# Norm stages of a four-layer kernel: the copies of the turned features shared by VectorE and ScalarE, and one dummy product behind the turns instead of four

## Chip, cores and metric

One Trainium2 chip, one of its cores. The metric is the device time of one execution in microseconds. A time without anything said is counted from the start of the profiled execution's span.

## What is computed

The input is 4 sequences of 256 tokens with 256 features in float32. Four layers follow each other, and each one has the same frame:

```python
xn = _layernorm(x, axis=-1)
s = _Lk_attn_ref(xn, ...)
g = _silu(_Lk_ffn_ref(xn, ...))
x = x + s * g
```

The mixers are, in order, a gated linear recurrence, a selective scan, a 16-head attention and a latent attention; the feed-forward parts are a mixture with 8 experts, a squared-relu network with a layer norm, a mixture with 16 experts and capacity 128, and a network with 4-bit weights. Only the layer norm ahead of layer 0 and of layer 2 is touched here. It takes each token's mean and variance over its 256 features, `(x - m) / sqrt(v + 1e-5)`.

## The kernel before, in words

The 1024 tokens lie as 8 tiles (`NT`) of 128 tokens, one token on a partition (`x_tok`, `xn_tok`). The products need the features on the partitions, so each norm also makes `xnT`, two tiles (`KD`) of 128 features by 1024 tokens, worked on in two halves of 512 tokens.

`norm_stage` (line 78) is called four times: by layer 0 (first norm), layer 1 (second, with `rms_to`, which makes a second scaled and turned copy), layer 2 (third) and layer 3 (fourth, with `beside`, a function that adds work on weights). The first and the third have neither. They are one block each, in which every engine has its own written-out program, and a block ends when all engines have reached its end (line 106 is where that shows up as a releaser in the trace).

- **SyncE** issues the layer's weight loads (lines 110 to 115) and waits for the first part of them (line 117). In the third norm these are four small loads it waits for and four later ones (`Wq`, `Wq_swap`, `cos`, `sin`), for which GpSimd waits in the stage behind.
- **VectorE** makes mean and variance from the statistics taken earlier (line 127), the reciprocal root with ScalarE's help (lines 129, 176, 131), and then the 8 normed token tiles (line 137).
- **TensorE** first runs two dummy products (line 155, `keep_busy` at line 239: a product of the identity with itself, 512 columns wide, whose result nobody reads; in float32 each is two instructions in the trace). Then it turns the 8 token tiles, two turns each, into four PSUM banks (line 160); the semaphore `turned` counts the tiles. Behind them come more dummy products (line 171): one in layer 0, four in layer 2.
- **ScalarE** waits for the first four turned tiles, copies two banks of 512 columns to `xnT`, waits for the other four and copies the other two (lines 182 to 186): four copies in all, in one queue.

`xnT_ready` is counted by these copies, but nobody waits for it: the stage behind reads `xnT` because the block has ended.

Behind the first norm comes `recurrent_layer_stage` (line 275), whose TensorE begins with the input product of `xnT` (line 506) and the router's small products (line 481). Behind the third comes `route_stage`: its TensorE begins with 16 instructions for the logits of 16 experts (line 1717), then the key product (line 1724), logits again, keys again, and then the queries (line 1699), which wait until GpSimd has turned the query weights by the position tables (lines 1658 and 1662). VectorE waits for the logits (line 1821) and then finds each token's experts. Its SyncE issues the next loads at once (line 1638 on).

Of the kernel before, what the change touches and what calls it, by code (L numbers as in the profile page):

```python
# [31 lines left out]
KD = D // P  # L32
HALF = N // 2
# [44 lines left out]
def norm_stage(nc, layer, x_tok, stats, xn_tok, xnT, ident, banks, loads, late=None, parity=False, issued=None, rms_to=None,  # L78
               beside=None):

    with ExitStack() as ctx:
        m = Core(nc, ctx).scope(ctx)
        mean_var = m.sbuf(f"mean_var{layer}", [P, NT, 2])
        var = m.sbuf(f"var{layer}", [P, NT])
        std = m.sbuf(f"std{layer}", [P, NT])  # L90
        rstd = m.sbuf(f"rstd{layer}", [P, NT])
        square = m.sbuf(f"mean_square{layer}", [P, NT])
        rms = m.sbuf(f"rms{layer}", [P, NT])
        norm_steps = nc.alloc_semaphore(f"norm_steps{layer}")
        var_ready = nc.alloc_semaphore(f"norm_var_ready{layer}")
        std_ready = nc.alloc_semaphore(f"norm_std_ready{layer}")
        square_ready = nc.alloc_semaphore(f"mean_square_ready{layer}")
        rms_ready = nc.alloc_semaphore(f"rms_ready{layer}")
        xn_ready = nc.alloc_semaphore(f"xn_ready{layer}")
        turned = nc.alloc_semaphore(f"xn_turned{layer}")  # L100
        xnT_ready = nc.alloc_semaphore(f"xnT_ready{layer}")
        rms_tok_ready = nc.alloc_semaphore(f"rms_tok_ready{layer}")
        rms_turned = nc.alloc_semaphore(f"rms_turned{layer}")
        loaded = nc.alloc_semaphore(f"weights_loaded{layer}")

        with nc.Block(no_gpsimd_drain=True) as block:

            @block.sync
            def _(sp):
                for dst, src in loads:  # L110
                    sp.dma_start(dst, src).then_inc(loaded, DMA)
                if late is not None:
                    for part, sem in zip(late[::2], late[1::2]):
                        for dst, src in part:
                            sp.dma_start(dst, src).then_inc(sem, DMA)
                if loads:
                    sp.wait_ge(loaded, DMA * len(loads))
                if issued is not None:
                    sp.wait_ge(*issued)
                if beside is not None:  # L120
                    beside["sync"](sp)

            @block.vector
            def _(dve):
                steps = Steps(dve, norm_steps)
                for t in range(NT):
                    steps.add(nc.vector.bn_aggr(mean_var[:, t, :], stats[:, t, :]))
                steps.join()
                nc.vector.tensor_scalar(var[:, :], mean_var[:, :, 1], EPS, None, ALU.add).then_inc(var_ready, 1)
                dve.wait_ge(std_ready, 1)  # L130
                steps.do(nc.vector.reciprocal(rstd[:, :], std[:, :]))
                if rms_to is not None:
                    steps.do(nc.vector.tensor_tensor(square[:, :], mean_var[:, :, 1], rstd[:, :], ALU.mult))
                    steps.do(nc.vector.tensor_tensor(square[:, :], square[:, :], rstd[:, :], ALU.mult))
                    nc.vector.tensor_scalar(square[:, :], square[:, :], EPS, None, ALU.add).then_inc(square_ready, 1)
                for t in range(NT):
                    nc.vector.tensor_scalar(
                        xn_tok[:, t, :], x_tok[:, t, :], mean_var[:, t, 0:1], rstd[:, t:t + 1],
                        ALU.subtract, ALU.mult).then_inc(xn_ready, 1)
                if rms_to is not None:  # L140
                    dve.wait_ge(rms_ready, 1)
                    steps.do(nc.vector.reciprocal(square[:, :], rms[:, :]))
                    dve.wait_ge(xn_ready, NT)
                    for t in range(NT):
                        nc.vector.tensor_scalar(rms_to[0][:, t, :], xn_tok[:, t, :], square[:, t:t + 1], None, ALU.mult
                                                ).then_inc(rms_tok_ready, 1)
                if beside is not None:
                    beside["vector"](dve)

            @block.tensor  # L150
            def _(pe):
                if beside is not None:
                    beside["tensor"](pe)
                else:
                    keep_busy(nc, banks[:, 7, :], ident, 2)
                for t in range(NT):
                    pe.wait_ge(xn_ready, t + 1)
                    for k in range(KD):
                        part = xn_tok[:, t, k::2] if parity else xn_tok[:, t, k * P:(k + 1) * P]
                        last = nc.tensor.transpose(  # L160
                            banks[:, KD * (t // 4) + k, (t % 4) * P:(t % 4 + 1) * P], part, ident[:, :])
                    last.then_inc(turned, 1)
                if rms_to is not None:
                    for t in range(NT):
                        pe.wait_ge(rms_tok_ready, t + 1)
                        for k in range(KD):
                            last = nc.tensor.transpose(banks[:, 4 + KD * (t // 4) + k, (t % 4) * P:(t % 4 + 1) * P],
                                                       rms_to[0][:, t, k * P:(k + 1) * P], ident[:, :])
                        last.then_inc(rms_turned, 1)
                elif beside is None:  # L170
                    keep_busy(nc, banks[:, 7, :], ident, 4 if layer else 1)

            @block.scalar
            def _(act):
                act.wait_ge(var_ready, 1)
                nc.scalar.activation(std[:, :], var[:, :], ACT.Sqrt).then_inc(std_ready, 1)
                if rms_to is not None:
                    act.wait_ge(square_ready, 1)
                    nc.scalar.activation(rms[:, :], square[:, :], ACT.Sqrt).then_inc(rms_ready, 1)
                if beside is not None:  # L180
                    beside["scalar"](act)
                for half in range(2):
                    act.wait_ge(turned, 4 * (half + 1))
                    for k in range(KD):
                        nc.scalar.activation(xnT[:, k, half * HALF:(half + 1) * HALF],
                                             banks[:, KD * half + k, :], ACT.Identity).then_inc(xnT_ready, 1)
                if rms_to is not None:
                    act.wait_ge(loaded, DMA * len(loads))
                    for half in range(2):
                        act.wait_ge(rms_turned, 4 * (half + 1))  # L190
                        for k in range(KD):
                            nc.scalar.activation(rms_to[1][:, k, half * HALF:(half + 1) * HALF], banks[:, 4 + KD * half + k, :],
                                                 ACT.Identity, scale=rms_to[2][:, k:k + 1])
# [45 lines left out]
def keep_busy(nc, bank, ident, count):  # L239

    for _ in range(count):
        nc.tensor.matmul(bank.rearrange("p (a b) -> p a b", a=BANK // P), ident[:, :],
                         ident[:, :].unsqueeze(1).broadcast_to([P, BANK // P, P]), start=True, stop=True)
# [2988 lines left out]
```

## Time and profile before

| | |
|---|---|
| median of 3 runs | 985.08 us |
| lowest and highest of them | 983.43 and 988.08 us |
| the profiled execution | 982.9 us |
| its span (first to last instruction) | 981.1 us |
| TensorE busy in the span | 902.4 us, 92% |
| VectorE, ScalarE, GpSimd busy | 666.2, 482.0, 331.2 us |
| mean granted clock of TensorE | 0.985 of full speed |

The profiled execution is a single one and lies 1.8 us outside its span and 2.2 us below the median of the three runs. PE is TensorE's products, PEld its weight loads, DVE is VectorE, ACT ScalarE, POOL GpSimd, SPq the loads and stores that SyncE issues. PEclk is the granted TensorE clock: 1.00 is 2.4 GHz, 0.50 is 1.2 GHz.

### The profile page before, as it was taken

To read this page: it belongs to the slowest core of one execution; us is meant where nothing else is said; L and a number is where in the kernel's file an instruction comes from. 1 tells how busy PE (TensorE), PEld (TensorE's weight loads), DVE (VectorE), ACT (ScalarE), POOL (GpSimd) and SP (SyncE) were. 2 spreads that over 40 slices of the span, in tenths; PEclk is the share of its full clock that TensorE was granted. 3 is DMA by queue.
4 is the path that set the end of the run, shared out by engine and by line. 5 is a ranking of instruction groups with operands and counts; after the bars stand their busy time and mean duration, and the time that the engine had idled before them with its cause. 6 is when DMAs were issued, how large, how long until landed. Compare 5 with 4: busy or idle time off the path is not lost. (4 is left out here: it accounts for less than half of the span.)

```text
span 981.1 us, 13728 instructions
## 1 busy us (share of the span) xinstructions
PE 902.4 (92%) x4683; PEld 557.6 (57%) x4683; DVE 666.2 (68%) x1109; ACT 482.0 (49%) x1043; POOL 331.2 (34%) x292
## 2 busy tenths in 40 slices
PE   6978689999999999989999899988899899999997
PEld 4566454365656556655565555566466556555554
DVE  4778667269999999875635565576786746666552
ACT  3566024799888788433134454556665630111112
POOL 0370700008888788623013242202554520000000
PEclk9999799999999999989999999999999999999999
DMA  7333224040000000018444444211000002111101
GB/s 215 100 100 100 84 82 135 0 116 27 27 29 23 16 28 1 2 40 237 118 149 111 98 108 97 32 43 33 12 1 1 2 1 65 33 32 32 33 0 43
DMA packets 63489, 59.01 MB, mean 60 GB/s; under 512 B 14960, under 2 KB 58192, under 8 KB 63424
## 3 DMA queue, kind: packets, MB, share of 16 engines
q1 hardware_dynamic: 56016, 47.02, 16.2%
q0 software_dynamic: 4944, 9.31, 4.8%
q10 hardware_dynamic: 2464, 1.84, 0.6%
q8 instruction: 37, 0.61, 0.3%
q14 instruction: 28, 0.23, 0.1%
HBM read 45.50 MB, written 9.50 MB: 56 GB/s over the span
## 5 line engine op out<-in xcount | busy, mean ns | idle before, releaser
L1290 POOL TENSOR_TENSOR seen<-state,c_row 128x512 f32<-128x512 f32 x128 | 160.6, 1275 | 100.5 <-DVE state L1310 72.5
L1310 DVE TENSOR_TENSOR_SCAN state<-decay,banks 128x512 f32<-128x512 f32 x128 | 154.7, 1215 | 14.1 <-issue 7.6
L2810 PE MATMUL banks<-xnT,weight 128*128 128x512 f32 x256 | 115.2, 592 | 0.0
L1248 ACT ACTIVATE weighed_x<-dx_tok,b_tok 128x512 f32<-128x512 f32 x124 | 87.7, 710 | 26.1 <-PE banks L1426 24.7
L2463 POOL TENSOR_TENSOR prob<-prob,inverse 128x512 f32<-128x512 f32 x64 | 65.2, 1039 | 95.4 <-DVE inverse L2581 95.4
L1258 ACT ACTIVATE decay<-delta_pairs,A 128x510 f32<-128x510 f32 x128 | 90.6, 708 | 6.2 <-DVE state L1310 6.2
L2816 ACT ACTIVATE w_WqT<-banks 128x512 f32<-128x512 f32 x32 | 19.1, 597 | 149.2 <-PE banks L2810 149.2
L1426 PEld LDWEIGHTS banks<-ident,weighed_x 128*128 128x128 f32 x512 | 58.3, 140 | 59.8 <-ACT weighed_x L1248 36.0
L1426 PE MATMUL banks<-ident,weighed_x 128*128 128x128 f32 x512 | 80.1, 279 | 2.1 <-DVE state L1310 1.1
L2810 PEld LDWEIGHTS banks<-xnT,weight 128*128 128x128 f32 x256 | 48.6, 190 | 48.3 <-issue 46.7
L1440 PE MATMUL banks<-seen,fold 128*64 128x512 f32 x256 | 69.0, 618 | 0.0
L2644 ACT ACTIVATE prob<-banks,shift 128x256 f32<-128x256 f32 x128 | 59.1, 471 | 18.7 <-DVE probT L2588 9.0
L2822 DVE TENSOR_TENSOR inter<-w_WqT,banks 128x512 f32<-128x512 f32 x32 | 22.0, 688 | 65.2 <-ACT w_WqT L2816 64.6
L2181 DVE COPY probT<-banks 128x512 f32<-128x512 f32 x48 | 33.1, 691 | 45.5 <-PE banks L2055 40.9
L2868 PE MATMUL banks<-weight,inter 128*128 128x256 f32 x256 | 60.4, 379 | 1.1 <-PEq L2446 1.1
L2868 PEld LDWEIGHTS banks<-weight,inter 128*128 128x128 f32 x256 | 48.5, 190 | 20.9 <-issue 15.8
L2576 DVE TENSOR_REDUCE shift<-banks 128x2 f32<-128x512 f32 x64 | 40.9, 680 | 19.5 <-PE banks L2504 19.5
L2588 DVE STREAM_TRANSPOSE probT<-prob 128x512 f32<-128x512 f32 x64 | 44.2, 701 | 11.7 <-POOL prob L2463 11.7
L2007 POOL DMA_INDIRECT y_dram<-slot_result,slot_target x16 | 25.3, 1582 | 77.8 <-ACT slot_result L2256 77.8
L2237 ACT ACTIVATE prob<-banks,score_shift 128x128 f32<-128x128 f32 (+1 forms) x128 | 44.4, 422 | 1.4 <-DVE score_shift L2177 1.4
L2504 PE MATMUL banks<-latT,q_now 64*128 64x256 f32 x256 | 36.3, 401 | 7.7 <-ACT prob L2644 7.7
L2177 DVE TENSOR_REDUCE score_shift<-banks 128x2 f32<-128x512 f32 (+1 forms) x48 | 32.8, 686 | 15.1 <-PE banks L2046 13.2
(440 smaller groups left out, 1724.7 us busy)
## 6 DMA issues: line engine op xcount, KB each, us to landing
c_row<-c_dram SPq DMA_DIRECT2D x32, 128.0 KB, 2.9
expert_rows<-expert_result SPq DMA_DIRECT2D x11, 256.0 KB, 2.1
slot_wide_w<-in_L_ffn_w_gate SPq DMA_DIRECT2D x16, 176.0 KB, 2.4
slot_wide_w<-in_L_ffn_w_up SPq DMA_DIRECT2D x16, 176.0 KB, 2.6
slot_down_w<-in_L_ffn_w_down SPq DMA_DIRECT2D x16, 176.0 KB
xn_dram<-xn_tok SPq DMA_DIRECT2D x2, 1024.0 KB, 6.2
gate_up_w<-in_L_ffn_gate_up_w SPq DMA_DIRECT2D x4, 512.0 KB, 7.1
delta_pairs<-conv_in SPq DMA_DIRECT2D x8, 256.0 KB, 3.6
```

What stands on the lines that cost most here:

```text
L1248: nc.scalar.activation(weighed[:, v % 2, tile, :, j, :], dx_tok[:, 4 * p + tile, :].rearrange("p (g e) -> p g e", g=groups), ACT.Identity, ...
L1258: nc.scalar.activation(decay[:, u % ring, :, 1:], delta[:, g, cols[p]].rearrange("p (b t) -> p b t", b=BATCH // 2)[:, :, 1:], ACT.Exp, sca ...
L1290: nc.gpsimd.tensor_tensor(seen[:, u % ring, :], state[:, u % ring, :], c_row[:, v % 4, :], ALU.mult).then_inc(seen_ready, 1)
L1310: nc.vector.tensor_tensor_scan(state[:, u % ring, :], decay[:, u % ring, :, :].rearrange("p b t -> p (b t)"), banks[:, 4 + u % 2, :], 0.0, ...
L1426: last = nc.tensor.transpose(banks[:, 4 + u % 2, tile * P:(tile + 1) * P], weighed[:, v % 2, tile, g, :, :].rearrange("p j e -> p (j e)"), ...
L1440: nc.tensor.matmul(banks[half, g // 2, :], fold[:, :], seen[:, u % ring, :], start=False, stop=(pair == STATES // 2 - 1), skip_group_check ...
L2237: last = nc.scalar.activation(dst[:, h, :], bank[:, h, :], ACT.Exp, bias=shift[:, u % 8, h:h + 1])
L2463: nc.gpsimd.tensor_tensor(two, two, inverse[:, u % 2, h, :].unsqueeze(2).broadcast_to([P, 2, SEQ]), ALU.mult).then_inc(prob_ready, 1)
L2588: nc.vector.transpose(probT[:, b % 2, h, unit, :], prob[:, u % 2, h, :]).then_inc(flipped, 1)
L2644: last = nc.scalar.activation(prob[:, u % 2, h, qt * SEQ:(qt + 1) * SEQ], score_bank(u, h)[:, qt * SEQ:(qt + 1) * SEQ], ACT.Exp, bias=shif ...
L2810: last = self.nc.tensor.matmul(self.banks[:, pair + j, :], self.weights.weight[:, s, j, k, tile * P:(tile + 1) * P], self.xnT[:, k, self.c ...
L2868: last = nc.tensor.matmul(banks[:, t // 2, (t % 2) * D:(t % 2 + 1) * D], jobs.inter[:, tile, t * P:(t + 1) * P], weight[:, s, 2, tile, :], ...
```

## The change

In the norms of layers 0 and 2 VectorE copies the second feature tile of each half, and ScalarE only the first. `keep_busy` behind the turns runs one dummy product in both of these norms; for layer 0 that is what it ran before. Norms two and four keep their programs.

```diff
+                elif beside is None:
+                    for half in range(2):
+                        dve.wait_ge(turned, 4 * (half + 1))
+                        nc.vector.tensor_copy(xnT[:, 1, half * HALF:(half + 1) * HALF], banks[:, KD * half + 1, :]
+                                              ).then_inc(xnT_ready, 1)
                 if beside is not None:
                     beside["vector"](dve)
...
                 elif beside is None:
-                    keep_busy(nc, banks[:, 7, :], ident, 4 if layer else 1)
+                    keep_busy(nc, banks[:, 7, :], ident, 1)
...
                 for half in range(2):
                     act.wait_ge(turned, 4 * (half + 1))
-                    for k in range(KD):
+                    for k in range(1 if rms_to is None and beside is None else KD):
                         nc.scalar.activation(xnT[:, k, half * HALF:(half + 1) * HALF],
                                              banks[:, KD * half + k, :], ACT.Identity).then_inc(xnT_ready, 1)
```

## Rows read from the trace of the kernel before

**Rows 1.** The page: busy time by engine, and the end chain by line.

```profile
PE 902.4 (92%) x4683; PEld 557.6 (57%) x4683; DVE 666.2 (68%) x1109; ACT 482.0 (49%) x1043; POOL 331.2 (34%) x292
PE banks L2810 10%; PE banks L2868 5%; DVE x_tok L258 0%; DVE gated L256 0%; ACT L235 0%; ACT gated L235 0%; ACT w_WqT L2816 0%; ACTq L2891 0%
```

**Rows 2.** Timeline, third norm: start, length (us), engine, line, operation, count [idle before, releaser].

```profile
434.37 3.75 PE L242 MATMUL banks<-ident 128*128 128x512 f32 x4 [4.33 <-PEq L2979]
...
437.81 0.43 SPq L115 DMA_DIRECT2D w_sin<-in_sin  x1
...
437.92 2.60 PE L160 MATMUL banks<-ident,xn_tok 128*128 128x128 f32 x16
...
439.69 2.07 ACT L185 ACTIVATE xnT<-banks 128x512 f32<-128x512 f32 x4 [4.23 <-PE banks L160]
...
440.36 3.60 PE L242 MATMUL banks<-ident 128*128 128x512 f32 x8
...
444.37 1.93 PE L1717 MATMUL banks<-w_gate_w,xnT 128*128 128x16 f32 x16 [0.41 <-PEq L106]
```

**Rows 3.** Timeline, first norm and what follows it.

```profile
11.43 2.52 PE L160 MATMUL banks<-ident,xn_tok 128*128 128x128 f32 x16
...
13.11 2.06 ACT L185 ACTIVATE xnT<-banks 128x512 f32<-128x512 f32 x4 [4.13 <-PE banks L160]
...
13.79 1.02 PE L242 MATMUL banks<-ident 128*128 128x512 f32 x2
...
15.54 1.10 PE L506 MATMUL banks<-xnT,w_W_in 128*128 128x512 f32 x2 [0.73 <-PEq L106]
```

**Rows 4.** One line, VectorE's copies out of PSUM: duration in ns, least/median/most.

```profile
L2181 DVE COPY probT<-banks x48: 680/692/692, 507.4 to 642.5; 128x512 f32<-128x512 f32 x48
```

**Rows 5.** Timeline, second norm: the turns, and ScalarE's second pair of copies.

```profile
142.63 2.71 PE L160 MATMUL banks<-ident,xn_tok 128*128 128x128 f32 x16 [0.35 <-DVE xn_tok L137]
...
145.37 1.08 ACT L185 ACTIVATE xnT<-banks 128x512 f32<-128x512 f32 x2 [0.21 <-PE banks L160]
```

**Rows 6.** Timeline, the stage behind the third norm.

```profile
445.48 1.26 POOL L1658 TENSOR_TENSOR w_Wq<-w_Wq,w_cos 128x512 f32<-128x512 f32 x1
...
448.04 1.26 POOL L1662 TENSOR_TENSOR w_Wq<-w_Wq,w_Wq_swap 128x512 f32<-128x512 f32 x1
...
449.84 0.29 DVE L1821 COPY logits<-banks 128x128 f32<-128x128 f32 x1 [4.90 <-PE banks L1717]
...
451.45 5.31 PE L1699 MATMUL banks<-xnT,w_Wq 128*128 128x512 f32 x12
```

**Rows 7.** DMA issues, 434 to 440 us: last figure is us from issue to landing.

```profile
w_sin<-in_sin SPq DMA_DIRECT2D x1, 128.0 KB, 4.5
w_before<-in_before SPq DMA_DIRECT2D x1, 64.0 KB, 2.0
```

**Rows 8.** Windows: length, busy us (instructions) of PE, PEld, DVE, ACT, POOL; PEclk, DMA share, GB/s.

```profile
142.60:147.70 5.10, 4.98 (x32) 3.22 (x32) 4.54 (x16) 3.15 (x6) 0.00 (x0) 1.00 1.09 317
147.70:149.80 2.10, 0.00 (x0) 0.00 (x0) 0.00 (x0) 1.44 (x3) 0.00 (x0) 1.00 0.43 128
...
430.00:432.50 2.50, 0.04 (x1) 0.00 (x0) 2.40 (x5) 0.00 (x0) 0.00 (x0) 1.00 0.00 0
...
434.30:439.30 5.00, 4.93 (x11) 2.78 (x12) 3.69 (x18) 0.21 (x1) 0.00 (x0) 0.50 0.58 149
439.30:443.90 4.60, 4.60 (x19) 2.40 (x17) 0.00 (x0) 2.07 (x4) 0.00 (x0) 1.00 0.19 59
...
500.80:504.20 3.40, 2.36 (x17) 1.35 (x18) 0.85 (x3) 1.88 (x2) 1.17 (x2) 1.00 0.63 207
504.20:507.60 3.40, 3.40 (x15) 2.13 (x12) 2.24 (x5) 2.44 (x9) 0.00 (x0) 0.50 1.02 289
...
108.50:121.50 13.00, 8.17 (x18) 6.05 (x19) 4.65 (x5) 1.17 (x2) 10.55 (x9) 0.50 0.31 90
...
15.50:19.30 3.80, 3.76 (x23) 2.84 (x23) 0.81 (x4) 3.17 (x5) 1.53 (x5) 1.00 0.76 235
```

## The prediction, as it was put on record

> **What bounds the kernel now.** I read the page first. TensorE is busy for 92% of the span and the chain that ended last is its own products in the last layer [rows 1], so a microsecond won in a norm stage reaches the end only if what follows simply starts earlier. Then I read the timelines of the two stages that the diff touches, to see which engine is the last to end in each, since a block ends only with its slowest engine.
>
> In the third norm it is TensorE, with work nobody needs. The turns run from 437.92 to 440.52, the four dummy products (eight instructions) from 440.36 to 443.96, and the next stage's first product starts at 444.37, 0.41 us behind their end, released by TensorE's own sequencer. ScalarE's four copies end at 441.76, 2.20 us before the dummies [rows 2]. Here the copies bound nothing yet.
>
> In the first norm it is ScalarE: its copies run from 13.11 to 15.17, while the one dummy there (two instructions) ends at 14.81; the next product starts at 15.54, 0.37 behind the copies [rows 3].
>
> **The change part by part.**
>
> *Third norm, three dummies less.* Eight instructions take 3.60 us from first start to last end [rows 2]; two take 1.02 at the same clock [rows 3]. TensorE then ends at 440.36 + 1.02 = 441.38. Alone this would move the end to ScalarE's 441.76 and save 443.96 - 441.76 = 2.20.
>
> *Third norm, copies shared.* The first pair starts together at 439.69. The second pair waits for the last turn. In the second norm the copy behind the last turn starts at 145.37, the turns having ended at 142.63 + 2.71 = 145.34 [rows 5], so I take 0.03 for the hand-over: the second pair starts at 440.55. VectorE's copy of the same shape out of PSUM takes 0.69 [rows 4], and these ran beside ScalarE's reads of other banks in the attention stage; it ends at 441.24. ScalarE's: four take 2.06 to 2.07 and two take 1.08, so a further copy adds 0.49 and one alone takes 1.08 - 0.49 = 0.59 [rows 2, 3, 5]; it ends at 441.14. Both are inside the dummy's 441.38, so TensorE still ends last. Saved: 443.96 - 441.38 = **2.58 us**.
>
> *First norm, copies shared.* The dummy stays as it was. Turns end at 11.43 + 2.52 = 13.95; second pair at 13.98; VectorE ends at 14.67, ScalarE at 14.57, the dummy at 14.81 [rows 3, 4]. The end goes from 15.17 to 14.81: **0.36 us**. Of that 0.04 goes again if the restart costs TensorE's 0.41 of rows 2 and not the 0.37 behind ScalarE; I leave it in, as it is less than the noise.
>
> *What the two added waits hold up.* VectorE's queue has nothing behind the copies in these blocks, and it is idle there today: 4.90 us of idle stands before its first needed read of the next stage [rows 6]. Nobody waits for `xnT_ready`. The cost is nothing unless the copy outlasts the dummy: VectorE has 441.38 - 441.24 = 0.14 us to spare. The nearest rows give 0.68 to 0.69 for it; were reading beside ScalarE to make it half as long again (1.03), the stages would lose 0.20 each, 0.4 together. That is the upper bound. A faster copy gains nothing, as the dummy ends later.
>
> *Loads.* SyncE's issues are unchanged and end at 437.81 + 0.43 = 438.24. The wait of line 117 ends with `w_before`, issued just before the four late ones: 2.0 us after its issue, so about 438, well before 441.38 [rows 2, 7]. The last late load, `w_sin`, is down at 437.81 + 4.5 = 442.3 [rows 2, 7]. GpSimd would reach the first product that needs these at 445.48 - 2.58 = 442.90 [rows 6], so 0.6 us are left; if that cover is gone, TensorE's queries still don't feel it at once, since GpSimd's last step ended at 449.30 and the queries began at 451.45, 2.15 us later [rows 6]. The stage's own loads are issued from its start and move with it. No DMA is added, removed or passed by another.
>
> *What is late next.* Behind both norms everything counts from the stage's start: TensorE's queue runs on without a gap into the queries, and VectorE waits for the logits [rows 6]. So the 2.58 and 0.36 should come through.
>
> *The clock.* The removed dummies held TensorE busy through the block's end. The clock was at 0.50 until 439.3, after an idle stretch that began at 430.04, and came back to 1.00 in the middle of the turns. It stayed there. It has also fallen behind a stretch with small work and idle in it, 500.8 to 504.2, and was low from 504.2 to 507.6 [rows 8]. With the change the stretch behind the turns is one dummy, 0.4 us of idle, and 1.9 us of products only 16 columns wide. The first norm has the same order already (turns, one dummy, 0.7 us idle, then input product and router), and there the row from 15.5 to 19.3 stands at 1.00 [rows 3, 8]. I take no fall. The second norm has 5.1 us of nothing but turns and then 2.1 us of idle, and the clock reads 1.00 in both [rows 8]: turns hold it. The Trainium skill, TensorE: Matmul & The Clock Gate, Part 4, says otherwise: turns don't count as busy the way products do and don't bring the full clock. By that rule the dummies are what held it, and the sum would be that of rival B. The rows of the second norm speak against it, as far as holding goes.
>
> *The sum.* 2.58 + 0.36 = 2.94 us. The profiled execution took 982.9, of which 981.1 is the span and 1.8 lies around it untouched: 982.9 - 2.94 = 980.0. It lay 2.2 below the median of the runs, so for the median 985.08 - 2.94 = **982.1 us**. That is 0.3%, less than the about 0.5% (4.9 us) that a measurement of this kernel can tell from no change.
>
> **The rivals.**
>
> *B, the clock falls once behind the third norm.* Place: the start of the next stage, logits and key product. For it: the fall at 504.2 behind thin work, and four dummies becoming one. Against: the first and second norm. Price: one low stretch of 3.4 us, in which TensorE does half its work, 1.7 us later. Net 2.94 - 1.7 = 1.24 faster: 983.8.
>
> *C, slower.* The same fall, but the clock doesn't return, as from 108.5 to 121.5 [rows 8]. 13.0 us at half rate cost up to 6.5; net 6.5 - 2.94 = 3.6 slower: 988.7. It decides from 5.9 us of low clock on, since half of that eats the 2.94. Against: between 108.5 and 121.5 TensorE was busy for 8.17 of 13.00, while behind the norm it has work without a gap (the queries follow at once, 5.31 us [rows 6]), and under such work it came back at 439.3.
>
> *D, the gain is hidden.* The next stage is paced by something that doesn't move (the query weights, or where its later loads meet others), or the copies don't start side by side, and most of 2.94 is waited for again: 985.1. For it: only 0.6 us stand between `w_sin` and its reader. Against: 2.15 us of slack behind that.
>
> *E, more is gained.* The shifted start makes another of the kernel's low-clock stretches fall away, such as 504.2 to 507.6: 1.7 more, 980.4. I see no reason for it to go this way and not the other.
>
> **How the numbers follow.** Forecast 0.68, B 0.14 (it takes in the page's rule), C 0.05, D 0.08, E 0.05. All but C lie within 4.9 us of 985.08, so it is the scatter of the runs (983.43 to 988.08) that may carry a verdict over the bound: I give faster by over 0.5% 0.09, which is a tenth of forecast and E and a little more, slower 0.04, most of it C, and no difference 0.87. Range: the forecast with the scatter of a median of few runs, 3 us below; above it B, D and 1 us: 979.0 to 986.0. That leaves out C and the tails.
>
> **What would show it.** In the third norm two instructions of line 242 behind the turns and not eight, ending near 441.4 if the norm starts at the same time; next product about 7.4 us after the norm's first dummy in place of 444.37 - 434.37 = 10.0. Two copies of VectorE of 0.69 beside two of ScalarE in each of both norms, ending before the dummy. In the first norm the input product at about 15.2. PEclk 1.00 for the 5 us behind the third norm. Wrong: a gap before line 1699 with the query weights as releaser (D); copies of 1.0 us; or a window of 0.50 just behind the third norm (B), a long one (C).

## The result and the profile after

The changed kernel takes 975.3 us at the median of ten runs (974.1 to 981.9), against 983.7 for the kernel before in ten (979.1 to 988.1). The means of these tens are 977.3 and 983.4. The ratio is 0.9938, interval 0.9909 to 0.9967: 0.6% faster, where 0.3% was forecast, and below the stated range. The profiled execution took 974.1 us with a span of 972.3, against 982.9 and 981.1.

| | before | after |
|---|---|---|
| span of the profiled execution | 981.1 us | 972.3 us |
| mean granted clock in it | 0.985 | 0.990 |
| DVE and ACT busy | 666.2, 482.0 us | 668.3, 480.2 us |

The timeline of the third norm after the change, with the columns of [rows 2]:

```profile
430.24 3.25 PE L247 MATMUL banks<-ident 128*128 128x512 f32 x4 [4.33 <-PEq L2984]
...
433.28 2.35 PE L165 MATMUL banks<-ident,xn_tok 128*128 128x128 f32 x16
...
434.79 0.60 ACT L190 ACTIVATE xnT<-banks 128x512 f32<-128x512 f32 x1 [3.46 <-PE banks L165]
434.79 0.69 DVE L150 COPY xnT<-banks 128x512 f32<-128x512 f32 x1 [0.52 <-PE banks L165]
435.46 1.02 PE L247 MATMUL banks<-ident 128*128 128x512 f32 x2
435.67 0.60 ACT L190 ACTIVATE xnT<-banks 128x512 f32<-128x512 f32 x1 [0.28 <-PE banks L165]
435.67 0.69 DVE L150 COPY xnT<-banks 128x512 f32<-128x512 f32 x1 [0.18 <-PE banks L165]
...
436.90 1.93 PE L1722 MATMUL banks<-w_gate_w,xnT 128*128 128x16 f32 x16 [0.41 <-PEq L106]
```

The lines are five further down than before. Both copies of a half start at the same moment, the second pair ends at 436.36, and the dummy ends last, at 436.48. From the first dummy behind the turns to the next stage's first product it is 436.90 - 435.46 = 1.44 us; before it was 444.37 - 440.36 = 4.01 [rows 2]. That is 2.57 us less; 2.58 was forecast.

The first norm after the change, answering to [rows 3]:

```profile
11.26 1.91 PE L165 MATMUL banks<-ident,xn_tok 128*128 128x128 f32 x16
13.01 1.02 PE L247 MATMUL banks<-ident 128*128 128x512 f32 x2
14.45 1.10 PE L511 MATMUL banks<-xnT,w_W_in 128*128 128x512 f32 x2 [0.41 <-PEq L106]
```

From the dummy's start to the input product it is 1.44 us, before 15.54 - 13.79 = 1.75: 0.31 less (0.36 forecast, of which 0.04 was said to go again with the dearer restart). And the copies cost what they cost elsewhere (duration in ns, least/median/most):

```profile
L150 DVE COPY xnT<-banks x4: 691/692/692, 12.3 to 435.7; 128x512 f32<-128x512 f32 x4
```

So the two stages give 2.57 + 0.31 = 2.88 us, as worked out (2.94), while the two spans differ by 8.8. Following the same instructions through both traces, the changed execution is 1.1 us ahead behind the first norm, 3.7 from 76 us on, 4.1 in layer 1, 7.5 behind the third norm, and 8.8 from 506 us on, where it stays. A stretch of the trace in which the granted clock is 0.50 is called a low stretch below. What is more than 2.88 lies in four places. In the first norm the same two dummies ahead of the turns (four instructions) took 3.37 us in place of 3.75. In the third the clock came back earlier in the norm's work, and the low stretch that began at 504.2 us before [rows 8] isn't there:

```profile
430.80:434.20 3.40, 3.40 (x9) 1.75 (x8) 3.05 (x12) 0.21 (x1) 0.00 (x0) 0.50 0.57 122
434.20:436.90 2.70, 2.29 (x15) 1.49 (x14) 1.46 (x3) 1.23 (x3) 0.04 (x1) 1.00 0.67 195
...
439.00:446.00 7.00, 7.00 (x29) 4.07 (x28) 3.01 (x17) 1.49 (x4) 2.95 (x3) 1.00 0.90 282
490.00:503.00 13.00, 11.26 (x62) 7.04 (x60) 6.82 (x20) 7.27 (x21) 3.67 (x4) 1.00 0.66 208
```

These windows of the changed kernel (columns of [rows 8]) show one low stretch of 3.4 us in the norm, where before it lasted to 439.3, and 1.00 through the start of the attention stage. The fourth place is the first expert stage, where TensorE waited less for gathered rows: from the first turn of such rows to the last product of that stage it is 47.4 us, where this profile of the kernel before has 51.7. That part is the lot of one execution, since two of the four profiles of the kernel before that were taken in all have 47.4 there too.

Two profiles can't tell luck from effect, so the experiments count many executions. Each one gives its mean clock beside its time, and from that the time spent at the lower clock: (1 - clock) x 2 x span, called **low time** below. Within every kernel the time goes with it, 0.51 us for each us of low time (all kernels fitted together, each about its own mean; 0.4 to 0.7 in a single one). 0.50 is taken below, and time less 0.50 x low time is called the **work**. All timed executions are counted in the means, while the ratios leave out those over 1.5% above their kernel's fastest (one of before, one of copies only, two of no dummy behind).

### The profile page after: what moved, and what is told of

It is laid out like the page before. It is cut to its first block and busy times, and to the rows that moved or that the text cites. A ratio compares the mean times of both kernels' runs of the same rounds, so it can differ in the third digit from the quotient of the medians.

```text
span 972.3 us, 13716 instructions
## 1 busy us (share of the span) xinstructions
PE 895.9 (92%) x4677; PEld 553.2 (57%) x4677; DVE 668.3 (69%) x1113; ACT 480.2 (49%) x1039; POOL 331.0 (34%) x292
## 5 line engine op out<-in xcount | busy, mean ns | idle before, releaser
L1431 PEld LDWEIGHTS banks<-ident,weighed_x 128*128 128x128 f32 x512 | 58.3, 140 | 59.8 <-ACT weighed_x L1253 36.0
L2012 POOL DMA_INDIRECT y_dram<-slot_result,slot_target x16 | 25.3, 1582 | 77.8 <-ACT slot_result L2261 77.8
```

The source lines that it names most:

```text
L1431: last = nc.tensor.transpose(banks[:, 4 + u % 2, tile * P:(tile + 1) * P], weighed[:, v % 2, tile, g, :, :].rearrange("p j e -> p (j e)"), ...
```

## The experiments

Errors are one standard error of the mean; each row has 12 executions, the kernel before 117 (three series of 35, and 12 that ran as an experiment of its own), the change 22 (the ten of the result and 12 more). The ratio is to the kernel before, run in the same series.

| kernel | mean us | low time | work | ratio, interval |
|---|---|---|---|---|
| before | 985.0 ±0.3 | 33.7 ±0.5 | 968.2 ±0.1 | |
| the change, both series | 978.6 ±0.7 | 26.9 ±1.1 | 965.2 ±0.2 | 0.9938 and 0.9946 |
| copies only | 983.8 ±1.5 | 31.3 ±2.3 | 968.1 ±0.4 | 0.9973, 0.9938 to 1.0009 |
| dummies only | 979.3 ±1.3 | 25.3 ±1.9 | 966.6 ±0.4 | 0.9941, 0.9906 to 0.9975 |
| five dummies | 983.8 ±0.8 | 29.1 ±1.7 | 969.2 ±0.5 | 1.0001, 0.9979 to 1.0023 |
| eight dummies | 989.4 ±0.7 | 35.6 ±1.4 | 971.7 ±0.3 | 1.0053, 1.0029 to 1.0076 |
| delay later | 984.0 ±0.9 | 29.5 ±1.8 | 969.3 ±0.5 | 1.0003, 0.9980 to 1.0027 |
| cover the gap | 983.3 ±0.9 | 30.6 ±2.0 | 968.0 ±0.4 | 0.9994, 0.9970 to 1.0018 |
| third norm only | 980.1 ±0.9 | 27.2 ±1.7 | 966.5 ±0.3 | 0.9950, 0.9926 to 0.9975 |
| no dummy behind | 982.7 ±1.8 | 35.7 ±3.9 | 964.8 ±0.4 | 0.9946, 0.9910 to 0.9982 |
| hold before norm | 981.7 ±1.0 | 29.4 ±1.5 | 967.0 ±0.4 | 0.9956, 0.9929 to 0.9983 |
| hold and cover | 982.3 ±0.9 | 28.3 ±1.8 | 968.1 ±0.2 | 0.9966, 0.9938 to 0.9994 |

**Copies only**: the change with `keep_busy(..., 4 if layer else 1)` kept.

```diff
-                    keep_busy(nc, banks[:, 7, :], ident, 1)
+                    keep_busy(nc, banks[:, 7, :], ident, 4 if layer else 1)
```

> The shared copies alone, with four dummy products kept behind the turns of the third norm. Theory 1 (the change is worth what the two norm stages show, the rest of the profiled difference is the lot of two executions): only the first norm gains, 0.4 us, ratio 0.9996; in the third norm the dummies still end last. Theory 2 (an earlier start of the first expert stage lets it run with less waiting for gathered rows, whatever the clock does): 0.4 us from the norm and 2 to 3 us more between 40 and 75 us of the span, ratio near 0.997.

Measured: work as before within 0.4, where theory 2 asked for 2.4 us less or more. The ratio tells nothing here, as its interval holds both theories' figures. So theory 2 is not borne out.

**Dummies only**: the kernel before with one dummy.

```diff
-                    keep_busy(nc, banks[:, 7, :], ident, 4 if layer else 1)
+                    keep_busy(nc, banks[:, 7, :], ident, 1)
```

> One dummy product in place of four, copies all by ScalarE. Theory 1: ScalarE's copies end last in the third norm, 2.2 us less, ratio 0.9978, the first norm as before. Theory 2: the same 2.2 us, as the first expert stage starts as before. Theory 3 (fewer dummies also change what the clock does behind the third norm, in the attention stage): 3.5 us or more, ratio 0.9964 or lower, with no stretch of 0.50 near 504 us.

Measured: 0.9941, as much as the whole change. The means are 6 us apart where the norm shows 2.3 (1.75 us from the dummy's start to the next stage, before 4.01), and the work is 1.6 ±0.5 less. In the profile there is no low stretch near 504 us. Theories 1 and 2 lie just outside the interval (0.9978 against 0.9975), 3 is met.

**The change again** and **before again** have no edit:

> The changed kernel once more, for more executions. Theory 1: the mean over these is about 3 us below that of before (ratio 0.997), and the six microseconds of the first comparison shrink. Theories 2 and 3: it stays near 6 us (ratio 0.994). In either case its times should fall into two groups about 6 us apart that go with the mean granted clock.

> The kernel before against itself: the ratio should be 1.000 within its interval, and the interval tells how much of a difference ten executions can tell at all. Its times, like those of the changed kernel, should go with the mean granted clock: about 0.5 us more for each us at the lower level.

The change gave 0.9946 (0.9919 to 0.9973), a mean of 979.7 and a median of 980.15: 5.6 us below the before of that series, so its 6 us hardly shrink. Its times did not fall into two groups, as was expected; they are spread from 974.8 to 983.4. The kernel before against itself gave 1.0013 (0.9985 to 1.0042), so some 0.3% is what 12 executions tell. The split over all executions: means 985.0 - 978.6 = 6.4 us; work 968.2 - 965.2 = 3.0; low time 33.7 - 26.9 = 6.8, which at 0.50 is 3.4. The forecast sum (2.94) is the work. The rest is the clock's.

Two of the profiles make the cleanest pair, as their low stretches up to the third norm are the same to 0.1 us: copies only (four dummies) and the change again (one). Timelines of the third norm, copies only:

```profile
441.45 3.60 PE L247 MATMUL banks<-ident 128*128 128x512 f32 x8
445.46 1.93 PE L1722 MATMUL banks<-w_gate_w,xnT 128*128 128x16 f32 x16 [0.41 <-PEq L106]
```

and the change again:

```profile
441.48 1.02 PE L247 MATMUL banks<-ident 128*128 128x512 f32 x2
442.92 1.93 PE L1722 MATMUL banks<-w_gate_w,xnT 128*128 128x16 f32 x16 [0.41 <-PEq L106]
```

445.46 - 442.92 = 2.54 us. This distance holds without a change up to 505 us. Then the windows of copies only

```profile
505.30:508.70 3.40, 3.40 (x16) 1.95 (x13) 2.34 (x5) 2.45 (x9) 0.00 (x0) 0.50 1.01 296
508.70:512.00 3.30, 3.30 (x20) 1.99 (x18) 1.53 (x3) 1.51 (x6) 0.00 (x0) 1.00 0.97 306
```

show a low stretch, and those of the change again, 2.5 us earlier at each instruction, none:

```profile
496.00:510.00 14.00, 12.13 (x65) 7.73 (x64) 7.82 (x21) 7.70 (x22) 3.86 (x4) 1.00 0.67 208
```

Behind it the distance is 3.82 us and stays so (spans 982.2 and 978.4). The low stretch cost 1.28.

Why should dummies 60 us ahead decide that? The attention stage starts thinly: TensorE idles 1.0 us for gathered rows, turns two tiles, and then works on 32 of 128 rows. In the kernel before:

```profile
501.85 0.44 PE L2108 MATMUL banks<-ident,slot_x 128*128 128x128 f32 x2 [1.04 <-DMA slot_x<-xn_dram,slot_token]
502.22 1.13 PE L2039 MATMUL banks<-keys,q 32*128 32x256 f32 x8
```

The guess is that the clock falls there or not by the moment at which this comes, and that the dummies set the moment. That is theory B of the next four runs.

**Five** and **eight dummies**:

```diff
-                    keep_busy(nc, banks[:, 7, :], ident, 4 if layer else 1)
+                    keep_busy(nc, banks[:, 7, :], ident, 5 if layer else 1)
```

> Five dummy products behind the turns of the third norm in place of four, nothing else. Theory A (each dummy costs its time and no more): 0.86 us slower, ratio 1.0009. Theory B (the four dummies put the thin start of the attention stage, an idle us and then products on 32 rows, at a moment at which the clock falls; any shift of about a us avoids that): the low stretch that begins near 504 us is gone as in the three profiles with one dummy, mean time at the lower level 4 to 6 us less than the kernel before, and the time 1.5 to 2.5 us LESS in spite of more work, ratio 0.998.

```diff
-                    keep_busy(nc, banks[:, 7, :], ident, 4 if layer else 1)
+                    keep_busy(nc, banks[:, 7, :], ident, 8 if layer else 1)
```

> Eight dummies in place of four. Theory A: four times 0.86 = 3.4 us slower, ratio 1.0035. Theory B: the shift of 3.4 us is as long as the shortest low stretch of the traces (3.4 us), to whose length the clock's changes keep within one execution, so the thin start meets the same moment as with four: the low stretch of the attention stage is there again, and the time is 3.4 us more too. Together with five dummies it tells whether place or amount decides: by A the two differ by 2.6 us, by B by 5 to 6.

Three more dummies, from five to eight, cost 5.7 ±1.0 us; their own time is 2.6. The work is 2.5 more and the low time 6.5, which at 0.50 is 3.2. With five, the stage's windows have no low stretch:

```profile
500.00:515.00 15.00, 13.82 (x101) 9.23 (x100) 6.12 (x17) 6.54 (x19) 2.90 (x3) 1.00 0.52 162
```

With eight it is back, 2.3 us behind the first turn of gathered rows (509.97), as it was 2.3 behind it (501.85) with four:

```profile
502.00:512.30 10.30, 9.27 (x82) 6.80 (x82) 2.32 (x11) 3.07 (x4) 2.91 (x3) 1.00 0.24 76
512.30:515.70 3.40, 3.40 (x15) 2.14 (x12) 2.24 (x5) 2.45 (x9) 0.00 (x0) 0.50 1.00 294
```

Against before (984.0 in that series) five dummies came out even: work +1.3 us and low time -3.2 us, which at 0.50 is 1.6 less. By A it would have been 0.9 slower, by B 1.5 to 2.5 faster with 4 to 6 us less low time; it lies between, and only the pair of five and eight tells A from B.

**Delay later** puts the shift elsewhere, at line 1746:

```diff
-                keep_busy(nc, banks[:, 1, :], ident, 2)
+                keep_busy(nc, banks[:, 1, :], ident, 3)
```

> Four dummies behind the turns as before, but three in place of two ahead of the shared experts' last products in the stage behind the third norm (line 1746), 17 us before the attention stage: the same shift of 0.86 us at another place. Theory A: 0.86 us slower. Theory B: as with five dummies, the low stretch near 504 us is gone and the time is 1.5 to 2.5 us less, ratio 0.998. Theory C (the number of dummies behind the turns acts on the clock itself, whatever their place in time): the low stretch stays.

The profile is that of five dummies to 0.1 us (span 985.1 and 985.2), without the low stretch, and so are mean and low time. It is the place in time and not what stands behind the turns, so theory C doesn't fit; the 1.5 to 2.5 us gain did not come here either.

**Cover the gap** puts one dummy behind the last product of the shared experts:

```diff
                     if t % 2:
                         last.then_inc(y_done, 1)
+                keep_busy(nc, banks[:, 1, :], ident, 1)
```

> The kernel before with one dummy product behind the shared experts' last product, where TensorE idles 1.0 us until the first gathered rows are there. The idle ahead of line 2108 shrinks to about 0.4 us and the start of the attention stage moves by at most 0.3 us. Theory B: the stretch is no longer thin enough, the low stretch near 504 us is gone, 1.5 to 2.5 us less, ratio 0.998. Theory A: 0 to 0.3 us more.

Its timeline: the dummy fills the idle, the turn comes 0.41 behind it.

```profile
499.87 1.02 PE L242 MATMUL banks<-ident 128*128 128x512 f32 x2
501.31 0.41 PE L2109 MATMUL banks<-ident,slot_x 128*128 128x128 f32 x2 [0.41 <-PEq L1630]
```

No low stretch in that stage, but one from 783.3 to 786.7, and the time is 0.7 ±1 us less: the sign of B, too small to be told from nothing.

**Third norm only** leaves the first norm as it was:

```diff
-                elif beside is None:
+                elif beside is None and layer:
                     for half in range(2):
                         dve.wait_ge(turned, 4 * (half + 1))
...
-                    for k in range(1 if rms_to is None and beside is None else KD):
+                    for k in range(1 if rms_to is None and beside is None and layer else KD):
```

> The change in the third norm alone; the first norm keeps its four copies by ScalarE (it has one dummy either way). Theory B (2.94 us of work, and the low stretch of the attention stage moved away): 0.36 us of the work stays, so the time with the clock's part taken out (time less half of the us at the lower level) is 0.4 above the changed kernel's 964.7 and 2.5 below the 967.6 of before, and the low time is as short as the changed kernel's, near 27 us against 33. Theory D (the first norm's earlier end shortens the first expert stage too): the gain over before shrinks by 2 us or more against the changed kernel.

It gives 0.9950 with the change's low time (27.2), so most of the gain is the third norm's. Its mean is 1.5 ±1.1 us above the change's and its work 1.3 ±0.3, where the first norm's rows show 0.31; what the other microsecond is stays open. That is less than the 2 us of theory D and more than the 0.4 of B, so D is not borne out at its size and not excluded in kind. (The two levels of work in the expectation lie some 0.5 below the table's; it is their difference that is compared.)

**No dummy behind** has none behind the turns in either norm:

```diff
-                elif beside is None:
-                    keep_busy(nc, banks[:, 7, :], ident, 1)
```

> The changed kernel with no dummy product behind the turns of the first and third norm. Theory B: VectorE's copy ends last, 0.1 us ahead of where the dummy ended, so 0.2 us in all, within the scatter of the changed kernel (mean 978.6). Rival (the one dummy holds the clock up behind the third norm): a low stretch of 3.4 us at the start of the stage behind it, low time 3 us more and 1.5 us slower than the changed kernel.

The rival's fall came, and longer than the 3.4 us that it named: low time +8.8 ±4 over the change, and over 50 us in four of the 12 executions, which no execution of any other kernel here reaches. Without the two longest executions, which the ratio leaves out, the low time is +5.7 ±4 and the mean 981.1. Its windows behind the third norm:

```profile
438.70:442.10 3.40, 2.28 (x21) 2.07 (x20) 1.94 (x4) 2.26 (x3) 1.06 (x5) 1.00 0.35 116
442.10:455.80 13.70, 13.70 (x36) 8.54 (x36) 4.49 (x23) 1.61 (x4) 4.23 (x7) 0.50 0.94 292
```

Turns, 1.1 us of idle and thin logits products, and then the clock is down for 13.7 us of full work. Its work (964.8) is 0.3 ±0.4 below the change's, which agrees with the 0.2 us forecast; over all executions the clock takes more back (mean 4.1 ±2 us above the change), while the ratio (0.9946) does not tell the two kernels apart.

**Hold before norm** was to beat both kernels, with the idle ahead of the third norm filled:

```diff
-                keep_busy(nc, banks[:, 6, :], ident, 4)
+                keep_busy(nc, banks[:, 6, :], ident, 7)
```

> The changed kernel with seven dummy products in place of four at the end of layer 1 (line 1497), which fill TensorE's idle while VectorE adds up layer 1: 428.5 instead of 425.9 us of the changed kernel's span. Theory B: the clock no longer falls ahead of the third norm (no low stretch from 431 to 434), low time 3.4 to 6.8 us less than the changed kernel's 27, and the turns end up to 1.8 us earlier: 1.5 to 3 us faster than the changed kernel, ratio to before near 0.991. Rival: VectorE's work is what the norm waits for, the clock only matters to dummies: no gain over the changed kernel, ratio 0.9938.

**Hold and cover** adds the dummy of the gap to it:

```diff
                     if t % 2:
                         last.then_inc(y_done, 1)
+                keep_busy(nc, banks[:, 1, :], ident, 1)
```

> The same with one dummy more behind the shared experts' last product, in the idle us ahead of the attention stage. Theory B: like the run before it where the thin start falls at a good moment, and up to 2 us faster where it does not, since the low stretch of the attention stage then can't come: mean between 974 and 977. Rival A (dummies cost their time): 0.2 us slower than the run before it.

Both missed. In the windows of hold before norm the low stretch ahead of the norm is gone, and another stands behind it:

```profile
433.00:447.10 14.10, 11.94 (x50) 6.24 (x49) 9.76 (x31) 2.69 (x4) 1.78 (x6) 1.00 0.33 78
447.10:457.30 10.20, 10.20 (x25) 6.09 (x24) 4.18 (x21) 1.39 (x3) 3.56 (x4) 0.50 0.92 301
```

With cover it was from 442.4 to 445.8. Ahead of the norm the low clock had cost little: from VectorE's first normed tile to the start of the last turn it is 2.90 us here and 3.76 in the changed kernel. Behind it TensorE's queue runs without a gap, so there each slower product delays the next. Neither kernel is faster than the change.

**Four more profiles**, each of a single execution, two of the kernel before and two of the change, asked whether the stretch of the attention stage is always there before.

> One more profile of the kernel before. Theory B: a low stretch of 3.4 or 6.8 us begins within 3 us of the first turn of gathered rows (line 2108), as in all four profiles with four or eight dummies. If the time is only chance, it is there in about one of three.

> One more profile of the changed kernel. Theory B: no low stretch within 10 us of the attention stage's first turn, as in the three profiles with one dummy and full work.

> As the first look at the kernel before: the low stretch of the attention stage is there.

> As the first look at the changed kernel: the low stretch of the attention stage is not there.

The first one of the kernel before, windows around the first turn at 497.69:

```profile
496.30:499.70 3.40, 2.34 (x16) 1.04 (x14) 0.51 (x3) 1.88 (x2) 1.49 (x2) 1.00 0.64 199
499.70:506.50 6.80, 6.80 (x23) 4.23 (x22) 3.11 (x5) 3.04 (x12) 0.00 (x0) 0.50 1.00 310
```

The second one of the kernel before: not there, but behind the third norm, at the key product:

```profile
447.90:451.30 3.40, 3.40 (x6) 1.34 (x6) 0.00 (x0) 0.00 (x0) 2.92 (x3) 0.51 0.61 172
```

The changed kernel has none in either. So "there in every execution" is wrong. Every profile has a low stretch at the very end of its span. What the profiles hold of low clock between the third norm's turns and that one: before, four profiles: 3.4; 6.8 + 3.4; 6.8 + 3.4; 3.4 us, mean 6.8. The change, four profiles: none. The timed executions differ by 6.8 ±1.3.

**The moment, read from all profiles.** In 16 of the 18 profiles (all but the two with the idle ahead of the norm filled) a low stretch ends in the third norm, 0.7 to 1.3 us ahead of the start of the last turn. The time from its end to the first turn of gathered rows in the attention stage:

| profiles | us from the clock's return to the first turn | low stretch behind it |
|---|---|---|
| four dummies: copies only, before, its first further profile, before again | 62.4, 62.5, 62.8, 62.9 | yes |
| eight dummies | 65.9, which is 62.5 + 3.4 | yes |
| one dummy: the change (four), third norm only, dummies only | 59.8 to 60.7 | no |
| five dummies, delay later | 63.4, 63.5 | no |
| four dummies: the second further profile of before | 64.3 | no |
| no dummy | 66.5 | no |
| cover the gap, without the idle us | 62.8 | no |

Neither earlier nor later is better as such: 59.8 to 60.7 and 63.4 to 64.3 escape the fall, 62.4 to 62.9 between them and 65.9 behind them don't. So the second further profile of before is no exception to theory B: its low stretch at 447.9 pushed the thin start 1.4 to 1.8 us later than in the other profiles with four dummies, past the moment at which the clock fell. And cover the gap comes at that moment, but without the idle, and has no fall. By these rows it takes both, the moment and the idle, though the second rests on that one profile. The table was read after the last run, and none was made to test it.

## Why the prediction was wrong

- **What bounds the norms**: right. Dummies ended last in the third, copies in the first.
- **Dummies and copies, 2.58 and 0.36**: right, 2.57 and 0.31, and VectorE's copy took the 0.69 of [rows 4] beside ScalarE's, ending 0.12 us ahead of the dummy (0.14 forecast). The work of all executions differs by 3.0 ±0.2 us, the sum was 2.94.
- **Added waits, loads, query weights (D)**: right. Without a gap TensorE goes from the keys to the queries, 7.1 us behind the stage's start both before and after.
- **The clock** is the step that failed. "I take no fall" behind the norm holds in all four profiles of the change. But the step looked for a fall that the change could bring, and only behind the norm. The low stretch at 504.2 stood in its own rows [rows 8], at a thin start that the change moves by 2.6 us, and rival E put it at 0.05 with "no reason for it to go this way". In the pair of profiles it is worth 1.28 us (E said 1.7), and over all executions the clock's part is 6.8 x 0.50 = 3.4 us, more than the work's. E had the mechanism and too small a chance; more than half of the measured 6.4 us was missing because the clock's term was put at nothing.
- **The range** came from the scatter of three runs; with 3.4 us of unseen gain 975.3 lay 3.7 us below its end. How far outside it lay is in part luck: the 12 executions of the change again have a median of 980.15, inside the range, and the mean of all 22 is 978.6. The missing 3.4 us are not: 6.8 ±1.3 us of low time are clear of the noise.
- **Rival B** did not happen with one dummy and did with none. The rows from the second norm (turns, then idle, at 1.00) did not show that turns hold the clock: without the dummy a run of turns, idle and thin products was followed by 13.7 us at 1.2 GHz. The Trainium skill, TensorE: Matmul & The Clock Gate, Part 4, where turns don't count as busy the way products do, fits that run; the thin products behind them fit it as well, and no run here parts the two. Nor did four dummies always hold the clock there: in the last profile of the kernel before it fell at 447.9, behind four of them.

Settled: the work, and that the third norm's dummies set a moment which decides on low stretches up to 60 us later (five against eight, the same shift at another line, the pair, and the table of moments). Not settled: that this gain would last. It is a matter of where thin places fall, and a change of another stage that shifts the attention stage against the norm can undo it. Why five dummies and delay later, which avoid the fall as well, won only 3 us of low time over before and not 6.8, and why the clock fell at 447.9 in the last profile of the kernel before, was not found either.

## What to carry to other kernels

Cost a removed wait or dummy from the timeline, and then list the places behind it where the granted clock falls or TensorE is thin: a shift of the whole program moves each of them, and with low stretches of 3.4 us or more that can be worth as much as the work removed. Compare kernels of this kind by means over a dozen executions with the mean clock beside each, so that work and clock can be told apart; a single profile of each said 8.8 us for 6.4. And before the last dummy is taken from between turns and a block's end with thin products behind it, measure the kernel without it: here it gave 0.3 us of work, and in four of 12 executions over 50 us of low clock, where the kernel with that dummy had at most 33.

## What was not expected

Going from five to eight dummies cost 5.7 us, while going from four to five made no difference that could be told. And half-filled idle is not always better: filling the idle ahead of the third norm only put the low stretch behind it, where it lasted 10.2 us in one profile and 3.4 in the other.
